# The attention logits u of a small graph network: both triangles from two column tiles of TensorE in place of the full left and right squares

## What is computed

```python
adj_tri = jnp.triu(adj, k=1)
diag_mask = jnp.triu(adj, k=0) - adj_tri
for l in range(L):                                   # L = 2
    m_left = jnp.einsum('bsh,oh->bso', h, W_left[l])
    m_right = jnp.einsum('bsh,oh->bso', h, W_right[l])
    u_left = jnp.einsum('bih,bjh->bij', h, m_left) / temper
    u_right = jnp.einsum('bih,bjh->bij', h, m_right) / temper
    u = u_left * adj_tri + u_left * diag_mask + u_right * jnp.swapaxes(adj_tri, 1, 2)
    delta_exp_u = jnp.exp(u) * adj
    attention = delta_exp_u / (jnp.sum(delta_exp_u, axis=2, keepdims=True) + 1e-10)
    h_lin = jnp.einsum('bsh,oh->bso', h, W_lin[l]) + b_lin[l]
    h = jax.nn.relu(_layer_norm(jnp.matmul(attention, h_lin), ln_a[l], ln_b[l]))
```

## Time and profile before

| | |
|---|---|
| median of 3 runs | 2846.78 us (2846.2 to 2848.68) |
| profiled execution | 2846.03 us, its span 2844.2 us |
| PE | busy 2792.3 us (98%), 24768 matmuls |
| PE weight loads | busy 1793.3 us (63%) |
| DVE | busy 2447.5 us (86%), 8170 instructions |
| ACT | busy 1784.8 us (63%), 4107 instructions |
| POOL | busy 1497.1 us (53%), 1585 instructions |
| DMA | 112.18 MB, 39 GB/s on the mean |
| granted TensorE clock, mean | 0.992 |

### The profile page before, as it was taken

How to read it: one execution, slowest core, us unless ns; L and a number is a source line. 1 busy time by engine, 2 the same in 40 slices (tenths; PEclk the granted TensorE clock), 3 DMA queues, 4 the chain that set the end, 5 groups by cost and what they waited for, 6 DMA issues and landing times.

```text
span 2844.2 us, 69230 instructions
## 1 busy us (share of the span) xinstructions
PE 2792.3 (98%) x24768; PEld 1793.3 (63%) x24768; DVE 2447.5 (86%) x8170; ACT 1784.8 (63%) x4107; POOL 1497.1 (53%) x1585
## 2 busy tenths in 40 slices
PE   7999999999999999999999999999999999999996
PEld 3566666666666666666666666666666666666654
DVE  4788988888888889888888888898888888888986
ACT  4556676656666556766566666567665667665664
POOL 2555565455554455654555654556545556445543
PEclk9999999999999999999999999999999999999998
DMA  4011011100111100111010111001111101110000
GB/s 163 20 35 43 21 43 43 46 32 24 43 43 43 46 32 21 46 40 46 32 35 32 43 43 46 32 21 46 40 46 32 46 21 43 43 46 32 21 28 21
DMA packets 55972, 112.18 MB, mean 39 GB/s; under 512 B 4944, under 2 KB 37712, under 8 KB 55632
## 3 DMA queue, kind: packets, MB, share of 16 engines
q1 hardware_dynamic: 55632, 107.76, 11.1%
HBM read 82.58 MB, written 25.17 MB: 38 GB/s over the span
## 4 chain that ended last, share of the span: by engine, by line
PE 97%; DVE 1%; issue 1%; ACT 1%; DMA 0%; POOL 0%; SPq 0%; POOLq 0%; DVEq 0%; ACTq 0%
PE psum L1243 70%; PE psum L1253 11%; PE psum L1304 9%; PE psum L1397 4%; PE psum L1371 3%; DMA xTin<-xT 0%; DMA s<-weights 0%; ACT w L587 0%; ACT w_hi L527 0%; DVE st L962 0%; POOL hl_lo L387 0%; DVE w_lo L785 0%; DVE st L908 0%; POOL e L416 0%; DVE y L900 0%
## 5 line engine op out<-in xcount | busy, mean ns | idle before, releaser
L587 ACT ACTIVATE w<-s,nmax 128x128 f32<-128x128 f32 x1536 | 474.1, 391 | 1.3 <-DVE nmax L837 1.2
L1243 PE MATMUL psum<-hT_hi,w_hi 128*128 128x512 f16 x1152 | 438.3, 381 | 13.5 <-POOL hT_lo L379 11.6
L1243 PE MATMUL psum<-hT_lo,w_hi 128*128 128x512 f16 x1152 | 438.0, 380 | 0.0
L1243 PE MATMUL psum<-hT_hi,w_lo 128*128 128x512 f16 x1152 | 437.9, 380 | 0.0
L527 ACT ACTIVATE nT_hi<-psum 128x512 f16<-128x512 f32 x384 | 228.3, 595 | 239.8 <-PE psum L1243 239.8
L461 POOL TENSOR_TENSOR fold<-s 128x768 f32<-128x768 f32 x128 | 232.7, 1818 | 224.5 <-DVE nmax L837 139.6
L837 DVE CUSTOM_DVE_ANT_0 s<-psum,adj 128x128 f32<-128x128 f32 x1536 | 343.1, 284 | 2.9 <-PE psum L1371 0.8
L527 ACT ACTIVATE hl_hi<-hl_raw 128x384 fp32r<-128x384 f32 x256 | 133.1, 520 | 300.5 <-DVE hl_raw L817 300.5
L387 POOL TENSOR_TENSOR hl_lo<-hl_raw,hl_hi 128x384 fp32r<-128x384 f32 x256 | 252.6, 993 | 125.7 <-ACT hl_hi L527 125.6
L527 ACT ACTIVATE pT_hi<-psum 128x512 f16<-128x512 f32 x384 | 224.0, 595 | 75.1 <-PE psum L1253 72.9
L804 DVE SCALAR_TENSOR_TENSOR nT_lo<-psum,nT_hi 128x512 f16<-128x512 f32 x384 | 253.5, 683 | 16.1 <-ACT nT_hi L527 16.1
(11 more groups left out here) (133 smaller groups left out, 8136.5 us busy)
## 6 DMA issues: line engine op xcount, KB each, us to landing
xTin<-xT SPq DMA_DIRECT2D x32, 768.0 KB, 4.6
xres<-x SPq DMA_DIRECT2D x32, 768.0 KB, 4.7
out<-y SPq DMA_DIRECT2D x128, 192.0 KB, 1.9
adjn<-adj SPq DMA_DIRECT2D x32, 256.0 KB, 4.9
adjT_sb<-adjT SPq DMA_DIRECT2D x32, 256.0 KB, 5.1
adj<-adj SPq DMA_DIRECT2D x32, 256.0 KB, 2.8
x<-weights SPq DMA_DIRECT2D x4, 576.0 KB, 5.8
s<-weights SPq DMA_DIRECT2D x3, 576.0 KB, 6.2
```

Source lines behind the costliest of these rows:

```text
L587: last = nc.scalar.activation(w[:, m], s[b % 2][:, m], ACT.Exp, bias=nmax[b % 2][:, m:m + 1], scale=-1.0)
L1243: last = mm(dst, a, b, start=(i == 0), stop=(i == total - 1))
```

## The change

PE makes a 192-column strip for each half of u's rows j, in place of 256 columns for all of them. `nT_hi` and `nT_lo` now hold, for each graph, 128 columns of the right form and then 128 of the left one. Rows j 0 to 63 (weight columns 0 to 63) take moving columns 0 to 191: right for all i, left for i below 64. Rows 64 to 127 take columns 64 to 255: right for i from 64, left for all i. So the square blocks on the diagonal are made in both forms, the others in one. The two matmuls of a pair use 64 weight columns each, in two column tiles of the array, and write PSUM partitions 0 to 63 and 64 to 127.

DVE masks 384 columns in place of 512 and adds 128 in place of 256, in place in `uLR`. ACT's exponential becomes three instructions, each on 64 partitions, since the second half stands in another order. `mask` comes from an array `adjM` that the host lays out, by one POOL instruction on 768 columns (`mask_of`) ahead of `y2_power(p, 2)`, in place of two on 512 with that statement between them. The adjacency's DMA grows from 256 to 384 KB a group.

```diff
-        nT_hi, nT_lo = (sb(f"nT_{p}", [KB, 2, GROUP, TOK], f16) for p in ("hi", "lo"))
+        nT_hi, nT_lo = (sb(f"nT_{p}", [KB, GROUP, 2, TOK], f16) for p in ("hi", "lo"))
...
+            nc.gpsimd.memset(keep[:, HALF:TOK], 1.0 / TEMPER).then_inc(keep_ok, 1)
...
+            for own in (slice(0, HALF), slice(HALF, TOK)):
+                nc.gpsimd.tensor_copy(keep[own, 0:HALF], keep_right[own, own]).then_inc(keep_ok, 1)
+                nc.gpsimd.tensor_copy(keep[own, TOK:TRI], keep_left[own, own]).then_inc(keep_ok, 1)
+            pool.wait_ge(keep_ok, 5)
...
-                nc.gpsimd.tensor_tensor(mask[:, :, 0], adjT_sb[:, 1 - p.odd], keep_L, ALU.mult).then_inc(mask_ok.sem, 1)
...
-                nc.gpsimd.tensor_tensor(mask[:, :, 1], adjn[:], keep_R, ALU.mult).then_inc(mask_ok.sem, 1)
...
+                nc.gpsimd.tensor_tensor(mask[:], adjm[:], keep[:, None, :].to_broadcast([128, GROUP, TRI]), ALU.mult)\
+                    .then_inc(mask_ok.sem, 1)
...
-                pool.wait_ge(e_raw[l].sem, p.upto(e_raw[l], h + 1))
+                pool.wait_ge(e_raw[l].sem, p.upto(e_raw[l], 3 * (h + 1)))
+                if l == 0 and h == 0:
+                    pool.wait_ge(adjT_in.sem, adjT_in.upto(p.it, 16))
...
-                mask_left(p)
+                mask_of(p)
                 y2_power(p, 2)
-                mask_right(p)
...
-                    nc.scalar.activation(e[:, 2 * h:2 * h + 2], e[:, 2 * h:2 * h + 2], ACT.Exp).then_inc(e_raw[l].sem, 1)
+                    two = slice(2 * h, 2 * h + 2)
+                    first, second = slice(0, HALF), slice(HALF, TOK)
+                    for j, i, src in ((slice(0, HALF), slice(0, TOK), slice(0, TOK)),
+                                      (second, second, first), (second, first, second)):
+                        nc.scalar.activation(e[j, two, i], uLR[h][j, :, src], ACT.Exp).then_inc(e_raw[l].sem, 1)
...
-                nc.vector.tensor_tensor(uLR[h][:], bank(f"u{l}", h).rearrange("p (b r t) -> p b r t", b=2, r=2),
+                nc.vector.tensor_tensor(uLR[h][:], bank(f"u{l}", h)[:, 0:2 * TRI].rearrange("p (b c) -> p b c", b=2),
                                         mask[:, 2 * h:2 * h + 2], ALU.mult).then_inc(u_read[l].sem, 1)
...
-                nc.vector.tensor_tensor(e[:, 2 * h:2 * h + 2], uLR[h][:, :, 0], uLR[h][:, :, 1], ALU.add)\
+                nc.vector.tensor_tensor(uLR[h][:, :, 0:HALF], uLR[h][:, :, 0:HALF], uLR[h][:, :, TOK:TRI], ALU.add)\
                     .then_inc(u_sum[l].sem, 1)
...
-                    dst = bank(f"u{l}", h)[:, g * 256:(g + 1) * 256].rearrange("p (r t) -> p r t", r=2)
-                    terms = [t for k in range(KB) for t in split(
-                        hT_hi[l][:, k, b], hT_lo[l][:, k, b], nT_hi[:, k, :, b], nT_lo[:, k, :, b])]
-                    for i, (a, m) in enumerate(terms):
-                        last = mm(dst, a, m, start=(i == 0), stop=(i == len(terms) - 1))
+                    dst = bank(f"u{l}", h)[:, g * TRI:(g + 1) * TRI]
+                    for n in range(3 * KB):
+                        k, t = divmod(n, 3)
+                        a = (hT_hi, hT_hi, hT_lo)[t][l][:, k, b]
+                        m = (nT_hi, nT_lo, nT_hi)[t][:, k, b].rearrange("p r t -> p (r t)")
+                        for j in range(2):
+                            own = slice(HALF * j, HALF * (j + 1))
+                            last = mm(dst[own], a[:, own], m[:, HALF * j:HALF * j + TRI],
+                                      start=(n == 0), stop=(n == 3 * KB - 1))
                 last.then_inc(u_full[l].sem, 1)
```

More of the change, by code:

```diff
@@ L14 @@
 HCOL = FEAT + 2
+HALF = TOK // 2
+TRI = 3 * HALF
 TEMPER = float(FEAT) ** 0.5
@@ L28, in upto, with program @@
         return group * self.per_group + n
-def program(nc, x, xT, adj, adjT, weights, biases, ln_cols, ln_rows, out):
+def program(nc, x, xT, adj, adjT, adjM, weights, biases, ln_cols, ln_rows, out):
     f32, f32r, f16 = mybir.dt.float32, mybir.dt.float32r, mybir.dt.float16
@@ L47, in program @@
         keep_right = sb("keep_right", [TOK])
+        keep = sb("keep", [TRI])
         pw = sb("pw", [2, GROUP])
@@ L58, in program @@
         xres = sb("xres", [GROUP, FEAT])
-        adjn = sb("adjn", [GROUP, TOK])
+        adjm = sb("adjm", [GROUP, TRI])
         adjT_sb = sb("adjT_sb", [2, GROUP, TOK])
-        mask = sb("mask", [GROUP, 2, TOK])
+        mask = sb("mask", [GROUP, TRI])
         hT_hi, hT_lo = ([sb(f"hT{l}_{p}", [KB, GROUP, TOK], f16) for l in range(2)] for p in ("hi", "lo"))
-        nT_hi, nT_lo = (sb(f"nT_{p}", [KB, 2, GROUP, TOK], f16) for p in ("hi", "lo"))
+        nT_hi, nT_lo = (sb(f"nT_{p}", [KB, GROUP, 2, TOK], f16) for p in ("hi", "lo"))
         hl_raw = sb("hl_raw", [GROUP, FEAT])
         hl_hi, hl_lo = (sb(f"hl_{p}", [GROUP, HCOL], f32r) for p in ("hi", "lo"))
-        uLR = [sb(f"uLR{h}", [2, 2, TOK]) for h in range(2)]
+        uLR = [sb(f"uLR{h}", [2, TRI]) for h in range(2)]
         e = sb("e", [GROUP, TOK])
@@ L106, in program @@
         xt_hi, xt_lo = (signal(f"xt_{p}", KB) for p in ("hi", "lo"))
[L107 removed]
+        adjT_in, mask_ok = signal("adjT_in", 16), signal("mask_ok", 1)
         nl_full, nl_hi, nl_lo = ([signal(f"nl{l}_{p}", 2 * KB) for l in range(2)] for p in ("full", "hi", "lo"))
@@ L111, in program @@
         u_full, u_read, u_sum, e_raw, e_ok, e_hi_ok, e_lo_ok = (
-            [signal(f"{p}{l}", 2) for l in range(2)]
+            [signal(f"{p}{l}", 6 if p == "e_raw" else 2) for l in range(2)]
             for p in ("u_full", "u_read", "u_sum", "e_raw", "e_ok", "e_hi_ok", "e_lo_ok"))
@@ L137, in program @@
                                        "y2nmr_ok", "fin_ok"))
-        ld, w_hi_ok, w_lo_ok, const_ok, ones_ok, b_ok = (
-            sem(p) for p in ("ld", "w_hi_ok", "w_lo_ok", "const_ok", "ones_ok", "b_ok"))
+        ld, w_hi_ok, w_lo_ok, const_ok, keep_ok, ones_ok, b_ok = (
+            sem(p) for p in ("ld", "w_hi_ok", "w_lo_ok", "const_ok", "keep_ok", "ones_ok", "b_ok"))
         w_in = [sem(f"w_in{i}") for i in range(3)]
@@ L279, in _ @@
                 if m == 1:
-                    sp.dma_start(adjn[:], adj[0]).then_inc(adj_in.sem, 16)
+                    sp.dma_start(adjm[:], adjM[0]).then_inc(adj_in.sem, 16)
                     sp.dma_start(adjT_sb[:, 0], adjT[0]).then_inc(adjT_in.sem, 16)
@@ L309, in body @@
                         .then_inc(x_in.sem, 16)
-                    sp.wait_ge(mask_ok.sem, mask_ok.upto(it, 2))
-                    sp.dma_start(adjn[:], adj[bass.ds(it + 1, 1)].rearrange("g i b j -> i (g b) j"))\
+                    sp.wait_ge(mask_ok.sem, mask_ok.upto(it, 1))
+                    sp.dma_start(adjm[:], adjM[bass.ds(it + 1, 1)].rearrange("g j b c -> j (g b) c"))\
                         .then_inc(adj_in.sem, 16)
@@ L352, in _, with mask_of @@
             pool.wait_ge(ones_ok, 7)
-            def mask_left(p):
+            for own in (slice(0, HALF), slice(HALF, TOK)):
+                nc.gpsimd.tensor_copy(keep[own, 0:HALF], keep_right[own, own]).then_inc(keep_ok, 1)
+                nc.gpsimd.tensor_copy(keep[own, TOK:TRI], keep_left[own, own]).then_inc(keep_ok, 1)
+            pool.wait_ge(keep_ok, 5)
+            def mask_of(p):
                 if not p.nxt:
                     return
-                adj_in_of(p)
-                nc.gpsimd.tensor_tensor(mask[:, :, 0], adjT_sb[:, 1 - p.odd], keep_L, ALU.mult).then_inc(mask_ok.sem, 1)
-            def mask_right(p):
-                if not p.nxt:
-                    return
-                nc.gpsimd.tensor_tensor(mask[:, :, 1], adjn[:], keep_R, ALU.mult).then_inc(mask_ok.sem, 1)
-            def adj_in_of(p):
                 pool.wait_ge(adj_in.sem, adj_in.upto(p.it + 1, 16))
-                pool.wait_ge(adjT_in.sem, p.upto(adjT_in, 16))
                 if p.l0:
                     pool.wait_ge(u_read[1].sem, p.upto(u_read[1], 2))
+                nc.gpsimd.tensor_tensor(mask[:], adjm[:], keep[:, None, :].to_broadcast([128, GROUP, TRI]), ALU.mult)\
+                    .then_inc(mask_ok.sem, 1)
             def xt(p, k):
@@ L517, in head @@
                     xt(prologue, k)
-                mask_left(prologue)
-                mask_right(prologue)
+                mask_of(prologue)
             passes(pool, body, head)
@@ L561, in nl @@
                     lr, kb = divmod(c, KB)
-                    hi(p, nl_full[l], c, f"nl{l}", nT_hi[:, kb, lr], nl_hi[l], 1.0 / WSCALE)
+                    hi(p, nl_full[l], c, f"nl{l}", nT_hi[:, kb, :, 1 - lr], nl_hi[l], 1.0 / WSCALE)
             def hl(p, l, b):
@@ L809, in nl @@
                     lr, kb = divmod(c, KB)
-                    lo(p, nl_hi[l], c, f"nl{l}", nT_lo[:, kb, lr], nT_hi[:, kb, lr], nl_lo[l], 1.0 / WSCALE)
+                    lo(p, nl_hi[l], c, f"nl{l}", nT_lo[:, kb, :, 1 - lr], nT_hi[:, kb, :, 1 - lr], nl_lo[l], 1.0 / WSCALE)
             def hl(p, l, b):
@@ L1523 @@
     a, b = np.asarray(L0_gnn_ln_a), np.asarray(L0_gnn_ln_b)
```

(9 more changed lines are left out.)

4 lines of the change are left out of this document (1 added, 3 removed).

## The result

The changed kernel takes 2851.19 us, median of 20 runs (2849.78 to 2853.47), against 2846.88 us of the kernel before (20 runs, 2845.51 to 2849.01): a ratio of 1.0015, with a 95% interval of 1.0008 to 1.0021. It is 4.3 us slower where 12 us less were forecast. The profiled execution has a span of 2851.0 us, 6.8 more than that of before.

The account below looks back on a forecast made before the run. PE was taken to bound the kernel. Its shorter stream gave -33 us, waits on ACT in layers 0 and 1 gave +11 and +10, so -12 and 2835 us; range 2812 to 2885, likeliest case 2825 to 2841.

Parts of the forecast that it names:

- What bounds the kernel: Whole kernel: PE is busy 2599.98 of 2600 us, so a microsecond off its stream is one off the kernel.
- Price of a pair: Two column-tiled matmuls of 192 columns in u on PE: 84 ns, bounds 82 and 164.
- streams side by side: In u on PE, the two column tiles overlap almost wholly, as row tiles in scores do, at 2 ns more.
- visits: Changing PE's tiling around each of the 128 calls of u costs 0.10 + 0.09 = 0.19 us.
- loads hidden: In u on PE, each 64-column weight load takes about 27 ns, two fitting under the 84 ns of streams.
- Rivals C and D: Pair of u: loads pace it, 109 ns, 2882 us, chance 0.22; or streams don't overlap, 164 ns, 3009 us, chance 0.13.
- Three cost 0.30 + 0.19 + 0.19 = 0.68, 0.38 more per exp_u: On ACT, exp_u's three exponentials occupy 0.68 us, 0.38 more than the single one.
- The upper bound that I set: On ACT, exp_u's two small exponentials cost at most 0.28 us each, 0.56 more per exp_u.
- the second place: Layer 1: PE waits 0.31 us at po(2) for oT_hi and oT_lo behind exp_u, 31 passes, 10 us back.
- The other edits, at nothing: DVE's mask and add, nT's writes, POOL's mask, the larger DMA and the adjacency wait cost nothing.
- rival E: Little changes: pairs of 87 to 92 ns, or exponentials at the upper bound (+5); 2841 to 2860 us, chance 0.17.
- the first place: Layer 0: xT_hi 0.76 us later, 0.41 usable, so PE waits 0.35 at qk(0), 31 passes, 11 us back.

Follow-up runs that it names:

- pe_part_alone: Changed kernel with one exponential over 128 partitions per pair of batches instead of three, so part of the computation differs: 2814.55 us.
- short_pairs: Changed kernel with eight of the nine matmul pairs of a batch streaming only 64 columns, leaving out part of the sums: 2831.55 us.
- three_exps_one_start: Kernel before with two extra 128-column exponentials behind each of its own, all starting at partition 0: 2860.02 us.
- act_part_alone: Kernel before, PE's full matrices kept, with each exponential cut in three by partition halves as in the change: 2878.6 us.
- before_reordered: Kernel before with only ACT's layer 0 order changed, as in exp_ahead_l0: 2845.64 us, ratio 0.9996.
- exp_ahead_l0: Changed kernel with ACT's layer 0 reordered: exp_u(0,0) ahead of hl(0,1), the three x1t copies together, then exp_u(0,1): 2819.2 us.

## Why the prediction was wrong, step by step

**What bounds the kernel:** right. In pe_part_alone what left PE's stream left the kernel.

**Price of a pair, streams side by side, visits, loads hidden:** right. 82 ns (84 forecast), 0.10 and 0.10 us (0.10 and 0.09), with 0.03 more behind the first pair, which the forecast lacked. (Its 0.415 ns a column is the slope between the rows and gives 80 ns by itself; the 82 holds some 3 ns a matmul beside it that the forecast doesn't name.) Four calls a pass are worth 0.98 us, 32 passes 31 us; pe_part_alone measured 32.5, the forecast had 33. Rivals C and D are out. The pages that I had set against the row, TensorEngine Tiling (Array Packing) and TensorE: Matmul & The Clock Gate, section LDWEIGHTS, in the Trainium skill, give an estimate of 107 ns a pair; this trace shows 82, and short_pairs 31.

**"Three cost 0.30 + 0.19 + 0.19 = 0.68, 0.38 more per exp_u":** this is the step that failed. By durations it was right, as three_exps_one_start shows (0.70 a set, 0.32 us a pass at qk(0), where the forecast had 0.35). But the price was taken from instructions that all begin at partition 0, and I carried the overlap with the successor over to instructions that don't. The overlap is lost where the half changes: the set occupies 0.96 us, and 0.13 more are lost in front of the second. The upper bound that I set, 0.56 more, was too low too (0.66 for a set, with 0.13 once a pass beside it). At qk(0) this makes 1.46 us of lateness and a loss of 0.98, so the margin is 0.48 (0.41 forecast); three_exps_one_start gives the same, 0.80 late (1231.85 to 1234.23 where the earlier trace rows have 1.59) and 0.32 lost. 0.98 us a pass times 31 is 30 us, where 11 were forecast. The miss of the sum is 16 us: 19 too little here, 5 too much at the second place, 2 too much gain on PE.

**Second place, "it waits 0.31 us, in 31 passes: 10 us back":** 0.16 us, 5 us. In the changed kernel's pass:

```profile
1288.59 0.33 PE L1242 MATMUL psum<-w_hi,oT_lo 128*128 128x384 f16 x1
1288.90 0.34 PE L1242 MATMUL psum<-w_hi,oT_hi 128*128 128x384 f16 x1
```

0.31 us between starts where 0.16 is the price. The mechanism is there, but only together with PE's gain: in act_part_alone and three_exps_one_start, where PE comes later, nothing is lost. With sets of 0.96 us the forecast's own reckoning would have given more than 0.31, so another of its numbers was off, the start of exp_u. Relative to PE's last transpose of to(2) exp_u(1, 1) starts 0.26 us before it in the kernel before and 0.59 before it in the two kernels just named, in the median of 24 passes. ACT's run of work that leads to it begins with a copy that waits for DVE's hl_raw, in the kernel before:

```profile
1280.60 0.52 ACT L527 ACTIVATE hl_hi<-hl_raw 128x384 fp32r<-128x384 f32 x1 [1.40 <-DVE hl_raw L817]
```

DVE and GpSimd show why hl_raw moved. In the kernel before (DVE, then POOL):

```profile
933.00 0.50 DVE L869 SCALAR_TENSOR_TENSOR rs<-live,rs 128x12 f32<-128x12 f32 x1
933.42 0.15 DVE L923 SCALAR_TENSOR_TENSOR nmr<-mv,rstd 128x1 f32<-128x1 f32 x1
```

```profile
932.75 0.73 POOL L416 TENSOR_TENSOR e<-e,adjT_sb 128x256 f32<-128x256 f32 x1
```

and at the same place in the changed kernel:

```profile
936.62 0.17 DVE L868 SCALAR_TENSOR_TENSOR rs<-live,rs 128x12 f32<-128x12 f32 x1
```

```profile
936.90 0.73 POOL L413 TENSOR_TENSOR e<-e,adjT_sb 128x256 f32<-128x256 f32 x1 [0.65 <-ACT e L593]
```

A DVE instruction of 12 columns takes 0.50 us when GpSimd's multiply began 0.25 us ahead of it, and ends 0.02 us behind the multiply's end; it takes 0.17 us when the multiply begins later. In every one of 24 passes it is the long form in the kernel before, in before_reordered and in pe_part_alone, and the short one in the changed kernel, exp_ahead_l0, act_part_alone and three_exps_one_start, whose longer exponentials put the multiply off. So a later exponential made DVE's hl_raw and ACT's chain behind it 0.33 us earlier, and softened its own blow. In short_pairs the same instruction takes 0.31 us, and there another instruction of GpSimd was under way (DVE, then POOL):

```profile
926.60 0.31 DVE L868 SCALAR_TENSOR_TENSOR rs<-live,rs 128x12 f32<-128x12 f32 x1
```

```profile
926.29 0.60 POOL L458 TENSOR_TENSOR fold<-fold 128x192 f32<-128x192 f32 x1
```

Again it ends 0.02 us behind GpSimd's. All ten traces together have 1200 of these instructions between 100 and 2700 us. In 420 of them a GpSimd instruction was under way at the start, and every one of these ends 22 to 30 ns behind the end of that instruction; in the other 780 none was, and none of them takes over 0.2 us. The Trainium skill, SBUF — State Buffer, section SBUF: two separate sides, gives a rule that fits: VectorE with two inputs in SBUF and GpSimd share a port pair that one instruction holds to its end. No run here moved that instruction alone; what the ten traces show is that its length follows GpSimd's without an exception.

**The other edits, at nothing:** borne out; no wait on the mask, the adjacency or nT shows in PE's list, and pe_part_alone contains all of them.

**The sum as measured:** -31 + 30 + 5 = +4 us, against 4.3 between the medians. The result lies in my rival E by its size and by one of its two mechanisms, exponentials dearer than thought, at a price beyond the bound that I gave for them. That E's +5 comes so near is luck: it had 22 us at the first place and 16 at the second, and 30 and 5 were measured.

## What to carry to other kernels

An instruction cut into pieces by partitions costs more than its pieces: before you price such a cut, look for a neighbour in the trace that starts at the same partition, and if there is none, let the missing overlap (here 0.1 us for each change of half, to and fro) into the upper bound. When a change makes one engine faster and burdens another, read which transfers to the fast engine lie behind the burdened one's queue; here the change paid 28 us as soon as no exponential stood between the three copies that PE waits for, in an order that is worth nothing to the kernel before. Moving an instruction past a wait works only if the queue in front of it has no idle time to lose, as the same move in layer 1 showed.

## What the runs showed of the hardware

- ACT's instructions overlap by about 0.1 us (a copy of 597 ns and its successor start 0.49 to 0.50 us apart) unless the first partition moves between 0 and 64: then the distance is 0.62 us, and in 316 cases of one trace the successor begins 23 to 26 ns behind the end. For the exponentials it is 0.43 instead of 0.31 behind the large one. Reads from SBUF and writes are judged apart: a copy from PSUM in between does not give the overlap back to the next reader of SBUF. The Trainium skill states such a rule for VectorE alone (VectorE: DVE Perf Modes, section Two Vector instructions with no wait between them): an instruction whose operand starts in another group of 32 partitions than the last one in that memory begins when all earlier ones have finished. ACT agrees with it in this trace, with partitions 0 and 64, the only ones that it shows.
- Two column tiles of 64 columns run side by side at the price of one stream: 82 ns for twice 192 columns, 31 ns for twice 64. The two weight loads of a pair, 64 columns each, fit into those 31 ns.
- Going into column tiles and out of them costs 0.10 us each, about as for the row tiles in the earlier trace rows (0.10 and 0.09), and the pair behind the first comes 0.03 us later than the others.
- A DVE instruction of 12 columns with two inputs in SBUF takes 0.17 us by itself. When one of GpSimd is under way as it starts, it ends 22 to 30 ns behind that one's end and so lasts 0.30 to 0.97 us here.
